# Attention and expert layer on one core: all four weight scales made before the first block's steps, first score split moved from GpSimd to VectorE

## What is computed

```python
x = x + xattn(layernorm(x), ctx, ctx)      # one head: softmax(q k^T / sqrt(128)) v, with biases
h = layernorm(x)
probs = softmax(h @ router_w.T)            # 8 experts
k = argmax(clip(gelu(h @ w1.T + b1) @ w2.T + b2)) + 1     # 1..6
scores = where(rank(probs) < k, probs, 0)
for e in range(8):
    g, u = h @ gate_w[e].T, h @ up_w[e].T  # 336 hidden units
    out += scores[e] * ((silu(g) * u) @ down_w[e].T)
x = x + out
```

## Time and profile before

| | |
|---|---|
| runs | 786.17, 788.01, 787.82 us; median 787.82 us |
| profiled execution | 788.26 us, of which the span of instructions is 786.5 us |
| busy share of the span | PE 97%, DVE 79%, ACT 74%, POOL 72% |
| granted clock of PE, mean | 0.991 of full |

### The profile page before, as it was taken

One profiled execution on the slowest core, in us unless ns is written; L12 is line 12 of the kernel. 1 busy time (PEld: TensorE's weight loads), 2 busy tenths in 40 slices (PEclk: granted clock), 3 DMA queues, 4 the chain that ended last, 5 costly groups with the idle time before them and its releaser, 6 DMA issues.

```text
span 786.5 us, 13918 instructions
## 1 busy us (share of the span) xinstructions
PE 764.4 (97%) x3825; PEld 384.1 (49%) x3825; DVE 621.9 (79%) x1341; ACT 585.6 (74%) x1032; POOL 563.3 (72%) x629
## 2 busy tenths in 40 slices
PE   7779999999999999999999999999999999999997
PEld 4534445554545545454554545455454545544443
DVE  6679888787887878778787877878687786878765
ACT  5777877777777777777778777778777777777664
POOL 2876877868686776868668685876868587686763
PEclk9979999999999999999999999999999999999999
DMA  9000011102010110201101020110201001010100
GB/s 345 6 15 0 14 28 14 41 1 67 2 46 21 27 42 1 66 0 26 40 19 47 0 66 0 26 40 0 66 0 49 19 15 28 1 41 1 28 1 27
DMA packets 52382, 25.07 MB, mean 32 GB/s; under 512 B 32496, under 2 KB 51056, under 8 KB 52336
## 3 DMA queue, kind: packets, MB, share of 16 engines
q1 hardware_dynamic: 52048, 24.06, 11.9%
q10 hardware_dynamic: 288, 0.48, 0.2%
HBM read 12.73 MB, written 4.19 MB: 22 GB/s over the span
## 4 chain that ended last, share of the span: by engine, by line
PE 88%; DVE 4%; POOL 3%; issue 2%; ACT 2%; DMA 1%; POOLq 0%; DVEq 0%; ACTq 0%
PE bank L497 26%; PE bank L499 26%; PE bank L498 26%; PE bank L409 2%; PE bank L389 2%; POOL weighted L1025 1%; PE bank L493 1%; PE bank L398 1%; DVE bank L1313 1%; PE bank L482 1%; PE bank L375 1%; PE bank L454 1%; PE bank L467 1%; DVE hid_lo L1319 1%; PE bank L473 1%
## 5 line engine op out<-in xcount | busy, mean ns | idle before, releaser
L1025 POOL TENSOR_TENSOR weighted<-silu,score_bc 128x512 f32<-128x512 f32 x336 | 424.5, 1270 | 167.7 <-ACT silu L792 163.2
L1313 DVE SCALAR_TENSOR_TENSOR bank<-bank,h_scale,weighted 128x512 f32<-128x512 f32 x336 | 253.1, 753 | 122.7 <-PE bank L499 109.9
L786 ACT ACTIVATE hid_hi<-bank 128x512 f16<-128x512 f32 x336 | 200.6, 597 | 145.7 <-DVE bank L1313 144.7
L792 ACT ACTIVATE silu<-bank,silu_scale 128x512 f32<-128x512 f32 x336 | 230.4, 686 | 24.2 <-PE bank L499 23.6
L1319 DVE TENSOR_TENSOR hid_lo<-bank,hid_hi 128x512 f16<-128x512 f32 x336 | 228.2, 679 | 11.8 <-ACT hid_hi L786 11.8
L497 PE MATMUL bank<-xn_lo,gate_hi 128*128 128x512 f16 x336 | 128.5, 382 | 0.9 <-POOL xn_lo L959 0.9
L497 PE MATMUL bank<-xn_lo,up_hi 128*128 128x512 f16 x336 | 128.3, 382 | 1.0 <-DVE hid_lo L1319 0.9
L497 PE MATMUL bank<-hid_lo,down_hi 128*128 128x512 f16 x336 | 127.5, 380 | 1.7 <-DVE down_lo L1140 1.5
L499 PE MATMUL bank<-xn_hi,gate_hi 128*128 128x512 f16 x336 | 128.4, 382 | 0.0
L498 PE MATMUL bank<-xn_hi,gate_lo 128*128 128x512 f16 x336 | 128.3, 382 | 0.0
L498 PE MATMUL bank<-xn_hi,up_lo 128*128 128x512 f16 x336 | 128.3, 382 | 0.0
(11 more groups left out here) (175 smaller groups left out, 831.3 us busy)
## 6 DMA issues: line engine op xcount, KB each, us to landing
x_in<-in_x SPq DMA_DIRECT2D x16, 256.0 KB, 2.9
out<-out_sb SPq DMA_DIRECT2D x16, 256.0 KB, 2.4
ctx_in<-in_ctx_t SPq DMA_DIRECT2D x14, 240.0 KB, 2.8
raw_gate<-in_gate_t SPq DMA_DIRECT2D x3, 448.0 KB, 6.4
raw_up<-in_up_t SPq DMA_DIRECT2D x3, 448.0 KB, 8.1
raw_down<-in_down_t SPq DMA_DIRECT2D x3, 448.0 KB, 10.0
out_sb<-in_ctx_t SPq DMA_DIRECT2D x2, 240.0 KB, 5.1
consts_sb<-in_consts ACTq DMA_DIRECT2D x1, 403.0 KB, 3.7
```

The costliest lines, as they stand in the source:

```text
L786: af(hid_hi[j % HRING][:], up_bank[j % U_BANKS][:], ACT.Copy).then_inc(hid_hi_ready, 1)
L792: af(silu[j % RING][:], gate_bank[(par + j) % G_BANKS][:], ACT.Silu, scale=silu_scale[:])\
L1025: g.tensor_tensor(weighted[j % RING][:], silu[j % RING][:], score_bc[par][:], ALU.mult)\
L1313: v.scalar_tensor_tensor(up_bank[j % U_BANKS][:], up_bank[j % U_BANKS][:], h_scale[:], weighted[j % RING][:], ALU.mult, ALU.mult).then_inc ...
```

## The change

- Round 0 covers only gate; round 1 covers up, down and the actor matrix, and is done in the prologue too. Round 1 uses bank `x0`, no longer `y_bank`.
- The statistics of gate and up are magnitudes on DVE (six `weight_magnitude` instead of two), and those of down remain sums on ACT, earlier in its list. Four `weight_sums` on ACT are gone. `W_TOP` of gate and up follows.
- `split_scores(0)`, three instructions on POOL, is two on DVE.
- POOL no longer makes `weight_high(3)` (ACT does); `value_bias(1)` stands behind `rank_over(0)`.
- The parts' low halves are made one to three steps nearer the front of block 0 (`LOW_AT`), their high halves four (`HIGH_AT`).

```diff
-HIGH_AT = {5: 4, 7: 5, 9: 6, 11: 7, 13: 8}
-LOW_AT = {2: 3, 6: 4, 8: 5, 10: 6, 12: 7, 14: 8}
+HIGH_AT = {1: 4, 3: 5, 5: 6, 7: 7, 9: 8}
+LOW_AT = {1: 3, 3: 4, 5: 5, 7: 6, 9: 7, 11: 8}
...
             def score_transposes(n):
                 pe.wait_ge(s16_ready, n + 1)
-                pe.wait_ge(below_ready, 2)
+                pe.wait_ge(w_chain, 4)
...
-                    if isinstance(t, int) and t == 0 and j == 2:
-                        weights_turned(1, 2, 4)
-                    if isinstance(t, int) and t == 0 and j == 4:
-                        weights_spread(1, 2, 4)
...
             gate(0, 0, 1)
+            weights_turned(1, 1, 4)
             pe.wait_ge(v_raw_ready, 2)
             values(4, 0, up_bank[2])
+            weights_spread(1, 1, 4)
...
             def weight_high(n):
                 k, cols = weight_part(n)
-                act.wait_ge(w_mul_ready, 1 if k < 2 else 2)
+                act.wait_ge(w_mul_ready, 1 if k == 0 else 2)
...
-            weight_sums(2)
+            norm1(1, 1, 0, 2)
             exps(0)
-            norm1(1, 1, 0, 2)
+            norm1(1, 1, 2, BB)
             turned_probs(0)
-            weight_sums(3)
-            weight_sums(4)
-            weight_sums(5)
-            norm1(1, 1, 2, BB)
+            weight_sums(6)
+            weight_sums(7)
...
             values(2, up_bank[2])
+            weight_sums(8)
             turned_x2(0)
...
-            def split_scores(n):
-                pool.wait_ge(score_ready, n + 1)
-                wait(pool, st_done, n)
-                g.tensor_tensor(score16[:, :, 0:EXPERTS], score[:], s_scale[:], ALU.mult).then_inc(s16hi_ready, 1)
-                g.tensor_tensor(score_up[:], score[:], s_scale[:], ALU.mult).then_inc(s16hi_ready, 1)
-                pool.wait_ge(s16hi_ready, 2 * n + 2)
-                g.tensor_tensor(score16[:, :, EXPERTS:], score_up[:], score16[:, :, 0:EXPERTS], ALU.subtract)\
-                    .then_inc(s16_ready, 1)
...
-            value_bias(1)
             weight_high(2)
-            weight_high(3)
             x2_low(0, 0)
...
             rank_over(0)
-            split_scores(0)
+            value_bias(1)
             value_bias(2)
...
+            def split_scores(n):
+                dve.wait_ge(score_ready, n + 1)
+                v.tensor_scalar(score16[:, :, 0:EXPERTS], score[:], S_SCALE, None, ALU.mult).then_inc(s16hi_ready, 1)
+                dve.wait_ge(s16hi_ready, n + 1)
+                v.scalar_tensor_tensor(score16[:, :, EXPERTS:], score[:], S_SCALE, score16[:, :, 0:EXPERTS], ALU.mult,
+                                       ALU.subtract).then_inc(s16_ready, 1)
...
+            weight_magnitude(5)
+            weight_tops(1, 1, 3)
             router_less(0)
             actor_logits(0)
             router_sum(0)
             row_sum(1)
+            weight_top(1, 1, 4)
             count_far(0)
             route_ahead(0)
             route_rank(0)
             count_first(0)
+            weight_scales(1, 1, 4)
             scores(0)
+            split_scores(0)
             weight_low(1)
             weight_low(2)
```

More of the change, by code:

```diff
@@ L122, in program @@
         w_max = sb("w_max", [P, 4])
-        w_top_col, w_one, w_top = sb("w_top_col", [2, 2]), sb("w_one", [2, P]), sb("w_top", [2, 2 * P])
+        w_top_col, w_one, w_top = sb("w_top_col", [3, 2]), sb("w_one", [3, P]), sb("w_top", [3, 2 * P])
         w_half = sb("w_half", [P, 4])
@@ L505, in weights_turned @@
                 else:
-                    pe.wait_ge(x2_ready, 2)
-                transpose((gate_bank[0], y_bank)[i][0:hi - lo, 0:P], w_max[:, lo:hi], ident_sb).then_inc(w_turned, 1)
+                    pe.wait_ge(below_ready, 2)
+                transpose((gate_bank[0], x0)[i][0:hi - lo, 0:P], w_max[:, lo:hi], ident_sb).then_inc(w_turned, 1)
             def weights_spread(i, lo, hi):
                 pe.wait_ge(w_top_ready, 2 * i + 2)
-                mm((gate_bank[0], y_bank)[i][:, P:P + hi - lo], w_top[0:hi - lo, i * P:(i + 1) * P],
+                mm((gate_bank[0], x0)[i][:, P:P + hi - lo], w_top[0:hi - lo, i * P:(i + 1) * P],
                    consts_sb[0:hi - lo, 0:hi - lo], start=True, stop=True).then_inc(w_spread, 1)
@@ L889, in _ @@
             nc.scalar.preload_act_table(ACT.Silu)
-            weight_high(1)
             gated(0, 0, 0)
@@ L893, in _ @@
             gated(0, 0, 1)
+            weight_high(1)
             score_copy(0)
@@ L898, in _ @@
             values(4, up_bank[2])
+            weight_high(3)
             keys(5)
-            weight_sums(6)
-            weight_sums(7)
-            weight_sums(8)
             turns(act, turn)
@@ L1123, in result_scale @@
                 dve.wait_ge(w_mul_ready, 2)
-                v.tensor_scalar(y_scale[:, 1:2], y_scale[:, 0:1], w_pow[:, 2:3],
-                                8.0 / (W_TOP[1] * W_TOP[2] * H_SCALE), ALU.mult, ALU.mult).then_inc(y_scale_ready, 1)
+                v.scalar_tensor_tensor(y_scale[:, 0:1], w_pow[:, 0:1], w_pow[:, 1:2], w_pow[:, 2:3], ALU.mult,
+                                       ALU.mult).then_inc(w_chain, 1)
+                dve.wait_ge(w_chain, 7)
+                v.tensor_scalar(y_scale[:, 1:2], y_scale[:, 0:1], 8.0 / (W_TOP[1] * W_TOP[2] * H_SCALE), None,
+                                ALU.mult).then_inc(y_scale_ready, 1)
             def actor_scales():
@@ L1362, in turn @@
                         aggregate_2(1)
-                        weight_tops(1, 2, 3)
-                    if isinstance(t, int) and t == 0 and j == 3:
-                        weight_top(1, 2, 4)
                     if isinstance(t, int) and t == 0 and j == 4:
-                        weight_scales(1, 2, 4)
                         result_scale()
@@ L1416, in _ @@
             weight_magnitude(0)
+            weight_magnitude(1)
             row_max(0)
@@ L1420, in _ @@
             row_sum(0)
-            weight_magnitude(1)
+            weight_magnitude(2)
             residual(0, 0, 0, BB)
@@ L1426, in _ @@
             aggregate_2(0)
-            weight_tops(0, 0, 2)
-            weight_top(0, 0, 2)
+            weight_tops(0, 0, 1)
+            weight_magnitude(3)
+            weight_top(0, 0, 1)
             norm2(0)
-            weight_scales(0, 0, 2)
+            weight_scales(0, 0, 1)
+            weight_magnitude(4)
             row_max(1)
```

15 lines of the change are left out of this document (7 added, 8 removed).

## The result

| | before | after |
|---|---|---|
| median of 5 runs each | 787.82 us (786.17 to 788.13) | 792.17 us (791.93 to 793.01) |
| profiled execution, of it the span | 788.26, 786.5 us | 792.49, 790.6 us |

The ratio is 1.0064, with a 95% interval of 1.0049 to 1.0079. The forecast was 788.9 us, with a range of 784.9 to 790.9.

A forecast was written before the change was run, and what follows sets the result against it. PE, busy for 97% of the span, was taken as the bound, with its waits and low clock in the first 100 us. 3.0 - 1.9 = +1.1 us gave 788.9 against 787.8 us, range 784.9 to 790.9.

The forecast's parts named there:

- (1): Router's chain up to rank_over(0): added scale instructions on ACT and DVE make it 1.5 us later.
- (2): Split on DVE: small instructions alternate with POOL's three value_bias; score_transposes starts 2.5 us later, at about 37.5.
- (3): From the transposes to values(5): PE's low clock may begin and end earlier in its work, gain 0.5 us.
- (4): ACT from values(5) to norm2(1): weight_high(4) adds 1.0 us to the chain; turn_x2(1) comes 3.0 us later, at 53.8.
- (5): Low halves of down made earlier: down_lo wait and two hid_lo waits go, gain 1.5 + 0.4 = 1.9 us.
- the loop is left as it is: Block loop: the change acts only on the start, where some 15 us can be saved at most.
- B: Rival, chance 0.25: DVE's split is not held up beside value_bias; transposes start at 34.6, -3.0 us, 784.8 us.
- C: Rival, chance 0.15: longer PE wait before the transposes keeps the clock low up to values(5); up to +4.7 us, 792.5.
- The sign of what would show me wrong: Transposes before 36, a hid_lo wait over 1 us at steps 8 to 12, or norm2(1) waiting for POOL's shift.
- the first part: Opening on what bounds the kernel: of the waits for w_top and norm2(1) the second ends last; removing w_top alone moves nothing.

The follow-up runs named there:

- run 1: Changed kernel with POOL waiting for the split scores before its three value_bias; 789.8 us, ratio 1.0027.
- run 2: Changed kernel with value_bias(1) back at its old place behind rstd_2(0); 790.49 us, ratio 1.004.
- run 3: Changed kernel with the split of the scores back on GpSimd, behind rank_over(0) and before the three value_bias; 789.61 us, ratio 1.0032.
- run 8: Kernel before, with high and low half of part 6 (down_lo) one step nearer the front; 787.88 us, ratio 1.0009.
- run 5: Kernel before, with only the split moved to VectorE and GpSimd waiting for it before value_bias(2); 786.74 us, ratio 0.9991.
- run 12: Changed kernel keeping only the scales; split, value_bias(1), HIGH_AT and LOW_AT as before; 789.63 us, ratio 1.0017.
- run 7: Changed kernel with low halves 5 and 6 at steps 8 and 9, 7 and 8 at 10 and 11; 789.97 us, ratio 1.0038.
- run 14: Changed kernel with three one-element memsets more among GpSimd's first instructions; 792.11 us, ratio 1.0056.
- run 6: Changed kernel with the low halves at the steps of before (LOW_AT); 790.54 us, ratio 1.0033.
- run 9: Changed kernel with weight_high(4) at step 2 in place of step 1; 793.32 us, ratio 1.0085.
- run 10: Changed kernel with POOL waiting for the split before its first value_bias and the low halves at the steps of before; 788.95 us, ratio 1.0023.

## Why the prediction was wrong, step by step

**(1) The router's chain, +1.5 us: right in size.** `al_far` starts at 32.42 (forecast 32.25), `rank_less` at 33.59 (33.4). Single executions scatter by more than that: `rank_less` starts between 33.05 and 35.78 in the profiles of all runs that have this prologue, and between 31.72 and 33.41 in those that have the one of before.

**(2) The split: right.** Forecast: transposes at 37.5; measured 37.62, behind three held-up DVE instructions (the forecast had `score` held up and the split's two behind one `value_bias`; it is the other way round, and the time is the same). Shown by runs 1, 2 and 3: from `rank_less` to the transposes 4.0 us with three `value_bias` beside it, 3.0 with two, 1.1 with none. By the Trainium skill (SBUF — State Buffer, section SBUF: two separate sides) a GpSimd instruction that reads SBUF and a VectorE instruction with two SBUF inputs or in a two-port mode lock each other out for the whole instruction; the trace agrees even for 3 elements a partition (`w_mul`, 1.10 us beside `value_bias`, 0.16 alone). Overlooked was that the changed kernel frees GpSimd's split of its own hold-up, so that the move cost 2.5 us against a split left where it was (run 3).

**(3) Clock after the transposes, -0.5: right, for these two executions.** The low level lasts from about 37 to 43.6 as against 35.6 to 42.4, and up to the value copy on ACT (47.15 against 44.97) 0.4 us of the 2.6 are won back. That the kernel before has a low stretch here at all belongs to the execution that was profiled: run 8 has the same wait and full clock. Runs 1, 3, 5 and 12 have full clock from 34 to 42 us too, behind waits of 0 to 1.1 us.

**(4) `turn_x2(1)`, +3.0: measured +3.6.** Of the 0.6 us more, 0.34 us is ACT's wait for `hidden(1)` in front of the second `high`; DVE starts it at 48.23, behind low half 3, which takes 2.04 us beside a `weigh` (1.14 alone). The text said that this half ends before it is asked for; it doesn't. The rest is 0.1 us each in (2) and (3), and rounding. In run 7 the same half isn't held up (1.12 us), and `turn_x2(1)` comes 16.0 us after the transposes in place of 16.7; but in run 14, with the half where the changed kernel has it, it is 17.6, so a difference of this size between two executions shows nothing. Unforeseen on the other side: the low clock behind `turn_x2(1)` lasts 2.9 us and not 5.3, -1.2.

**(5) The low halves, "Gain 1.5 + 0.4 = 1.9 us": this step failed.** The gain itself is there and larger (1.8 + 1.1 with the gaps). The sentence that failed is "I count 1.5 to 2 us between a `low` and the up tile or down tile that asks for it". I looked at the steps' own consumers, at 1.14 us a low half. But `actor_gelu(1)` stands behind the halves of steps 5 and 7 in DVE's list, and both are held up by GpSimd (`x2_low`, then `weigh`): 2.12 + 2.17 us. PE waits 2.0 us longer for the gelu, then runs 3.2 us at the low level (1.6 us). Runs 6 and 7 show it: with the halves behind the gelu both go, and 0.26 to 0.31% (2.0 to 2.4 us) come back. Instead of -1.9 the step gave -2.9 + 3.9 = +1.0 us. How the 3.9 us divide is of this execution: 1.2 us of the wait are the time that PE had won in (4), and the low stretch followed the waits of 2.15 to 2.17 us (changed kernel, runs 2 and 9) but not those of 1.4 to 1.7 us at the same place (runs 1, 3 and 14). From `turn_x2(1)` to 103 us the difference goes from 3.6 to 3.4 us; a gain of 1.9 us was forecast.

**Not foreseen: +0.7 us at the turns of the loop.** The text had "the loop is left as it is". TensorE's program there is the same, and every row between two turns has the same distance to the next; only the gap at the turn is longer. In the profiles it is there in the changed kernel and in all runs that keep its scales and its split on VectorE, and not where the split is on GpSimd, nor in the kernel before with the split on VectorE. What decides it is open; that GpSimd's program is longer does not (run 14).

**Sum.** Forecast +1.1; with +0.6 and -1.2 in (4), +2.9 in (5), +0.7 in the loop: +4.1, the difference of the spans. **The rivals:** B, no hold-up, is excluded by the rows of the split and by run 1. C named the right mechanism, a low clock, at the wrong place: it is behind the gelu's wait, not behind the transposes. The sign of what would show me wrong, a `hid_lo` wait over 1 us at steps 8 to 12, looked at PE's wrong neighbour as well.

**What each part costs**, by the runs: the scales 0.17% (run 12), the split 0.32% (run 3; 0.09% of it, 0.7 us, at the turns of the loop), the low halves 0.26 to 0.31% (runs 7 and 6); the sum is 0.75 to 0.8% and the whole 0.64%, within the intervals. That the scales gain nothing although a wait of 2.9 us disappears was foreseen in the first part: the wait for `xn_nat` ends last.

## What to carry to other kernels

Before you move an instruction forward on an engine that executes in order, list everything that stands behind it until its old place, in this block's work and in the next block's, and ask who waits for each; the instruction's own consumers are only one of them. Price each instruction of VectorE and GpSimd from rows in which the other is busy, whatever its size: here a low half cost 1.14 or 2.1 us, and three elements 0.16 or 1.1. And a new idle time of PE may cost more than its length: here 2.15 us of wait were followed by 1.6 us lost to low clock, and 1.4 to 1.7 us of wait at the same place by none. Before you read two profiles against each other, look how far apart they are already ahead of the change, and count from there.

## What was unexpected in the hardware

- A wait removed in front of TensorE often came back further on: with 2.1 us less (run 5) or 2.9 us less (run 1) from `rank_less` to the transposes, `turn_x2(1)` came 1.7 and 1.5 us earlier, and the launches gained 0.1% and 0.4%.
- The low clock comes in stretches of different lengths: 5.8, 2.9 and 3.2 us in the changed kernel, 6.8 and 5.2 before; the same wait of 2.2 us in front of the transposes was followed by 6.8 us of it before and by none in run 8. Executions of one kernel differ in them: the seven of run 10 spread from 787.33 to 790.15 us, and the profiled one, 787.83 us, had a mean clock of 0.996 where its slowest had 0.99.
- The turn of the block loop cost TensorE 0.3 us between two matmuls in some kernels and 0.7 us (first turn) and 0.4 us (later ones) in others, whose own instructions on TensorE are the same.
